# A two-layer graph network: the first table pair made and gathered by column halves

## The reference, cut to what matters

```python
h = jnp.maximum(_layernorm(x), 0.0)
# layer 1, n_f = h
feat = jnp.concatenate([n_f[edge_src], n_f[edge_dst]], axis=1)
e_hh = relu(feat[:256] @ W_hh + b_hh)
e_oo = relu(feat[256:1536] @ W_oo + b_oo)
e_ho = relu(feat[1536:] @ W_ho + b_ho)
logit = (concatenate([e_hh, e_oo, e_ho]) @ W_a + b_a)[:, 0]
alpha = softmax of logit over the edges of one dst        # segment_max, exp, segment_sum
z_f = segment_sum(alpha[:, None] * n_f[edge_src], edge_dst)
x = x + concatenate([relu([n_f, z_f][:128] @ W_hn + b_hn), relu([n_f, z_f][128:] @ W_on + b_on)])
# layer 2, h = relu(_layernorm(x)), c from the edge weights' sums and the degrees of the nodes
x = x + relu(((segment_sum(h[src] * c, dst)) * deg_in ** -0.5) @ W_1 + b_1)
```

## Time and profile before

| | us |
|---|---|
| median of 3 runs | 614.83 (609.78 to 616.64) |
| profiled execution, its own time | 611.59 |
| its span, first to last instruction | 609.6 |
| PE busy in the span | 541.2 (89%) |
| DVE busy | 417.3 (68%) |
| ACT busy | 213.3 (35%) |
| POOL busy | 163.8 (27%) |
| moved by DMA | 144.81 MB, mean 238 GB/s |

### The profile page before, as it was taken

How to read it: one execution, slowest core, us unless ns; L and a number is a source line. 1 busy time by engine, 2 the same in 40 slices (tenths; PEclk the granted TensorE clock), 3 DMA queues, 4 the chain that set the end, 5 groups by cost and what they waited for, 6 DMA issues and landing times.

```text
span 609.6 us, 7403 instructions
## 1 busy us (share of the span) xinstructions
PE 541.2 (89%) x2425; PEld 352.1 (58%) x2425; DVE 417.3 (68%) x744; ACT 213.3 (35%) x283; POOL 163.8 (27%) x157
## 2 busy tenths in 40 slices
PE   3868999999999979897339997898997999989996
PEld 2757888644444434342114444686665888868885
DVE  6948557447868799859397869755684277787134
ACT  3520427499463452100100157111444073216200
POOL 3110000177765375553267430000000101121000
PEclk9998999999999998999859999866998999999999
DMA  8975551599999999999969995140000736204002
GB/s 335 380 291 172 178 208 63 180 371 410 410 412 415 409 386 406 414 409 411 409 201 412 409 410 213 36 165 11 2 2 2 276 95 234 85 2 138 1 34 104
DMA packets 43780, 144.81 MB, mean 238 GB/s; under 512 B 5536, under 2 KB 5856, under 8 KB 43744
## 3 DMA queue, kind: packets, MB, share of 16 engines
q1 hardware_dynamic: 22000, 69.22, 30.9%
q0 software_dynamic: 18560, 67.13, 28.1%
q10 hardware_dynamic: 3184, 7.99, 3.5%
HBM read 131.70 MB, written 12.62 MB: 237 GB/s over the span
## 4 chain that ended last, share of the span: by engine, by line
PE 40%; DVE 24%; DMA 17%; issue 6%; POOL 5%; ACT 5%; DVEq 2%; ACTq 1%; POOLq 0%
PE banks L1080 19%; DMA rows<-table,ids_i 13%; PE banks L1243 7%; PE banks L1172 6%; DVE masked L791 5%; POOL rows L435 5%; DVE rows L769 5%; DVE rows L770 4%; PE banks L1260 3%; PE banks L1190 3%; DMA lift_row<-liftT 2%; ACT pick_src L553 2%; ACT pick_src L557 1%; DMA lift<-lift_row 1%; DVE stats L671 1%
## 5 line engine op out<-in xcount | busy, mean ns | idle before, releaser
L435 POOL DMA_INDIRECT rows<-table,ids_i x124 | 140.4, 1132 | 183.6 <-DMA table<-stage 86.4
L1100 PE MATMUL banks<-w_raw,fT_raw 128*128 128x512 f32 x384 | 168.4, 598 | 10.1 <-DMA w_raw<-in_L_gnn_W_hn_dram 3.9
L1100 PEld LDWEIGHTS banks<-w_raw,fT_raw 128*128 128x128 f32 x384 | 73.0, 192 | 104.9 <-issue 92.3
L769 DVE TENSOR_TENSOR rows<-rows 128x1024 f32<-128x1024 f32 x62 | 75.7, 1220 | 47.2 <-DMA rows<-table,ids_i 47.0
L681 DVE TENSOR_TENSOR w_lo<-w_raw,w_hi 128x1024 fp32r<-128x1024 f32 x40 | 48.4, 1223 | 57.1 <-ACT w_hi L484 47.5
L1080 PE MATMUL banks<-w_hi,fT_hi 128*128 128x512 f32 x200 | 78.7, 393 | 8.1 <-DVE w_lo L681 7.2
L1080 PE MATMUL banks<-w_lo,fT_hi 128*128 128x512 f32 x200 | 78.3, 392 | 0.0
L1080 PE MATMUL banks<-w_hi,fT_lo 128*128 128x512 f32 x200 | 78.3, 391 | 0.0
L770 DVE SCALAR_TENSOR_TENSOR rows<-rows,wa_rep 128x1024 f32<-128x1024 f32 x62 | 76.0, 1225 | 2.1
L1143 PE MATMUL banks<-w_raw,fT_raw 128*128 128x512 f32 x128 | 58.4, 619 | 19.5 <-DVE xf L823 19.5
L484 ACT ACTIVATE w_hi<-w_raw 128x1024 fp32r<-128x1024 f32 x40 | 41.7, 1056 | 86.9 <-PE banks L1080 72.9
(11 more groups left out here) (164 smaller groups left out, 619.1 us busy)
## 6 DMA issues: line engine op xcount, KB each, us to landing
w_raw<-in_L_gnn_W_ho_dram SPq DMA_DIRECT2D x16, 512.0 KB, 7.7
table<-stage SPq DMA_DIRECT2D x32, 256.0 KB, 7.6
w_raw<-in_L_gnn_W_oo_dram SPq DMA_DIRECT2D x16, 512.0 KB, 6.8
w_raw<-in_L_gnn_W_on_dram SPq DMA_DIRECT2D x16, 512.0 KB, 5.5
w_raw<-in_L_gnn_W_hn_dram SPq DMA_DIRECT2D x16, 512.0 KB, 6.7
w_raw<-in_L_gnn_W_hh_dram SPq DMA_DIRECT2D x16, 512.0 KB, 7.3
w_raw<-in_L_gnn_W_dram SPq DMA_DIRECT2D x8, 512.0 KB, 3.9
lift<-lift_row ACTq DMA_DIRECT2D x7, 512.0 KB, 8.0
```

Source lines behind the costliest of these rows:

```text
L435: pool.indirect_dma_start(out=rows[:, slot, side, :], out_offset=None, in_=table[kind][side], in_offset=bass.IndirectOffsetOnAxis(ap=ids_i ...
L769: step(dve.tensor_tensor(rows[:, r, 0, :], rows[:, r, 0, :], rows[:, r, 1, :], ALU.add))
L1100: ins = pe.matmul(bank[j][:, :], fT_raw[:, k, m * P:(m + 1) * P], w_raw[:, c % SLOTS, n * H:(n + 1) * H], start=(k == 0), stop=(k == K - 1))
```

## The change

**Halves.** Chunks c < 16 take other slices of W_ho: chunk c loads rows k*128 of both W_top and W_bottom, but one column half of each (`chunk_rows`). So bank j = 2m + n now holds node block m of side n, and unit 0 makes the left halves of both tables, unit 1 the right ones. ACT copies the even banks of both units, DVE the odd ones with the bias, and two semaphores (`evac_act`, `evac_dve`) replace `evac`. SP stores unit 0's eight copies twice, first to new tensors `table_left` (rows of 2 KB), then to the left columns of the tables.

**Sixteen left halves.** Tiles 0, 2, ..., 30 (`LEFT`) are gathered in two parts. Once `table_left` has landed, POOL gathers the left halves (32 gathers of 256 KB), DVE sums them into `left_logit` after its w_lo of chunks 12 to 15, at c = 16, and at c = 19. After unit 1 `fetch` goes through tiles 0 to 61 as before, but takes right halves for the sixteen (from the table seen as rows of 2 KB, with indices 2*id + 1), and `lift_chunk` adds `left_logit`.

**What moves for it.** `dst_rep` lies over `h_edge` instead of `rows` and has 4 places, so the loads of its chunks 4 to 7 go from ACT to POOL, each behind a `member` chunk, and the h_edge gathers stand behind the left gathers and all member builds. DVE builds four members for each c from 4 to 11. The split of the edge weights (`split3`, `dst_q`) goes to c = 8. The words are loaded once, 7 loads instead of 14, on DVE at c = 19 and on PE before the HH transposes. `EDGES_BY`, and the places of lifts and maxima, are new; TOP's banks 0 and 1 are kept at c = 47. Two of four `hn_lo` leave the second round of spans and stand behind `adjT_lo`.

```diff
     def chunk_rows(c):
+        if c < 2 * K:
+            half, k = c // K, c % K
+            return W_ho.rearrange("(s r) d -> r s d", s=2)[k * P:(k + 1) * P, :, half * H:(half + 1) * H]
...
-        ROWS, REPS = 5, 6
+        ROWS, REPS = 5, 4
...
+        table_left = [nc.dram_tensor(f"table_left{s}", [N, H], F32, kind="Internal").ap() for s in range(2)]
...
+        LEFT = range(0, 32, 2)
+        NL = len(LEFT)
+        ITEMS = [(i, 0) for i in LEFT] + [(i, 1 if i in LEFT else 2) for i in range(TE)]
+
         EDGES_BY = [0] * C_BOT
         for c in range(20, C_BOT):
-            if c < 28:
-                n = 2 * (c - 19)
-            elif c < 32:
-                n = 16 + c - 27
-            elif c < 36:
-                n = 20 + 2 * (c - 31)
+            if c < 36:
+                n = 36 * (c - 19) // 16
             elif c < 44:
-                n = 28 + 13 * (c - 35) // 8
+                n = 36 + 12 * (c - 35) // 8
             elif c < 52:
-                n = 41 + 5 * (c - 43) // 8
+                n = 48 + 6 * (c - 43) // 8
...
-        FETCH_AFTER = (26, 30, 35, 40, 45, 55, 61)
-        MAX_AFTER = (27, 32, 37, 42, 47, 57, 62)
+        FETCH_AFTER = (25, 29, 33, 38, 42, 47, 58)
+        MAX_AFTER = (27, 31, 36, 40, 44, 49, 61)
...
+                for j in range(8 if u == 0 else 0):
+                    evacuated(sp, j)
+                    sp.dma_start(table_left[j % 2][j // 2 * P:(j // 2 + 1) * P, :], stage[:, j, :]).then_inc(left_stored, 16)
                 for j in range(8):
                     e = 8 * u + j
-                    sp.wait_ge(evac, e + 1)
+                    evacuated(sp, e)
                     m, n = j // 2, j % 2
...
+            for r in range(REPS, NC):
+                pool.wait_ge(member_done, r - REPS + 1)
+                dst_rep_load(pool, r)
+            pool.wait_ge(left_stored, 16 * STAGE)
+            pool.wait_ge(words_ready, 1)
+            for k in range(NL):
+                fetch(k)
+            pool.wait_ge(member_done, NC)
             pool.wait_ge(h_out, 16)
...
-                fetch(i)
+                fetch(NL + i)
...
-                for j in range(8):
+                for j in range(0, 8, 2 if u < 2 else 1):
...
-            def edge(i):
-
-                r = i % ROWS
-                dve.wait_ge(row_in[r], (i // ROWS + 1) * 32)
-                step(dve.tensor_tensor(rows[:, r, 0, :], rows[:, r, 0, :], rows[:, r, 1, :], ALU.add))
-                dve.scalar_tensor_tensor(rows[:, r, 0, :], rows[:, r, 0, :], 0.0, wa_rep[:, :], ALU.max, ALU.mult,
-                                         accum_out=logit[:, i:i + 1]).then_inc(edge_done, 1)
+            def edge(k):
+
+                (i, part), r = ITEMS[k], k % ROWS
+                cols = slice(0, D if part == 2 else H)
...
+                dve.wait_ge(row_in[r], (k // ROWS + 1) * 32)
...
-            split3(w_col, ids_f[:, 2, :])
...
-            dve.wait_ge(words_ready, 1)
-            words = [dve.value_load(pair_word[0:1, q % WORDS:q % WORDS + 1], min_val=0, max_val=4096 ** 2 - 1)
-                     for q in range(2 * WORDS)]
...
+            early = {12: 3, 13: 6, 14: 9, 15: 12, 16: 14, 19: NL}
             for c in range(4, C_BOT):
+                if c == K + 3:
+                    evacuate(0)
                 if c not in RAW:
                     lo(c)
-                if c < 20:
-                    for part in (2 * (c - 4), 2 * (c - 4) + 1):
-                        build_member(part // B, part % B)
+                if c < 19:
+                    for k in range(early.get(c - 1, 0), early.get(c, 0)):
+                        edge(k)
+                if c - 4 < NC:
+                    for b in range(B):
+                        build_member(c - 4, b)
...
-                if c == C_HH + 3:
+                if c == C_TOP + 2 * K - 1:
                     keep_top(range(2))
...
+            pe.wait_ge(words_ready, 1)
+            words = [pe.value_load(pair_word[0:1, q:q + 1], min_val=0, max_val=4096 ** 2 - 1) for q in range(WORDS)]
+
             transpose_edges(0)
```

164 lines of the change are left out of this document (100 added, 64 removed).

## The result

The changed kernel takes 622.67 us (median of 11 runs, 617.39 to 628.09), the kernel before in the same comparison 616.44 (609.78 to 618.52, 11 runs): ratio 1.0099, 95% interval 1.0053 to 1.0145. It is slower by 1.0%, where 600.5 and faster were forecast. In all that follows a median is taken over all runs of a kernel, and a ratio over its fast runs alone, those within 1.5% of its fastest. The profiled execution took 625.53 us, span 623.6, against 611.59 and 609.6: 14.0 us more.

The account below looks back on a forecast made before the run. The middle was taken as bound twice: gathers fill the DMA engines, and DVE's order passes that to PE. Gains 6.3 + 3.1 + 3.5 less 1 of clock, 12 us off 611.6, plus 0.9: 600.5 us, range 588 to 612.

Parts of the forecast that it names:

- Step 1: DVE's early program: without word loads w_lo of chunk 4 starts at 34.8; PE's first pass ends at 62.4, not 71.
- Step 2: DVE's member builds and splitting: it copies its banks only at 65 us; left tables stand at 72.
- Step 3: Left gathers: 32 at 1.24 us; DVE's copies end at 117.4, before 115.6, so the 8.6 us gained are spent.
- Step 4: h_edge gathers beside the last table stores: second pass's first gather at about 126, plus 6.5 us (bounds 1.8 and 8).
- Step 5: Half rows in the second gather pass: 8.4 MB less gains 20.5 us; POOL's pace charged 3 us (bounds 0 and 7).
- Step 6: New tile counts in DVE's order: unit 3 copied at 236, HH starting at 308 instead of 314.35, 6.3 us sooner.
- Step 7: PE's seven word loads moved ahead of the transposes, where PE waits anyway: the 3.13 us before 377.49 go.
- Step 8: Span stage: DVE free when HH ends, and two hn_lo moved behind adjT_lo; counted as 3.5 of 4.6 us.
- Slower, the left gathers hold PE: Left gathers delay fT_raw and free banks, deciding from 1.67 us a gather; 621 us at 1.99; chance 0.08.
- Thin gain: POOL needs 1.43 us a gather in the left pass, 5.3 us more, and 2 more behind it: 608; chance 0.20.

Follow-up runs that it names:

- small parts alone: Kernel before with words loaded once and late, edge-weight split behind chunk 8, two hn_lo moved, no halves: 608.04 us, ratio 0.9899.
- the layout alone: Changed kernel without its left pass: whole rows everywhere, tile counts of before, the rest as changed: 609.07 us, ratio 0.9837.
- the changed kernel once more: Changed kernel run again without any edit, for a second profile: 624.05 us, ratio 1.0142.
- the left pass alone: Changed kernel gathering whole rows behind the second unit, of which DVE sums the right half for the sixteen tiles: 633.85 us, ratio 1.0266.
- one side left out: Kernel before, with tiles 0, 2, ..., 30 gathering only side 0 in whole rows: 605.70 us, ratio 0.9855.
- the run with POOL 4 tiles ahead: Half-row kernel with POOL at most 4 tiles ahead of DVE instead of 5, until tile 33: 609.36 us, ratio 0.9848.
- the free run with eight left halves: Changed kernel with left halves for tiles 0 to 14 only, h_edge gathers behind tile 40, no added pauses: 608.31 us, ratio 0.9901.
- with 4 tiles ahead: The free run with eight left halves, but POOL at most 4 tiles ahead of DVE until tile 19: 608.70 us, ratio 0.9900.
- the half-row kernel: Kernel before, tiles 0, 2, ..., 30 gathering and summing only left halves, right halves left out: 601.23, 619.69, 621.01, 624.56 us.
- 3 ahead, twice: POOL at most 3 tiles ahead of DVE instead of 5: half-row kernel 616.94 us (1.0057), changed kernel 634.92 us (1.0406).
- the pauses: Changed kernel with POOL waiting before tiles 6, 12, 18, 24 and 30 until DVE is 2 tiles behind: 635.61 us, ratio 1.0367.

## Why the prediction was wrong, step by step

The span was to fall by 12 and rose by 14.0. By the runs' medians the parts are: small parts and layout -6, left pass with the h_edge gathers behind it +25, half rows behind the turn -10, together +9, where the changed kernel itself measured +6.2 and +9.9. The runs of one kernel spread over 8 us and more, so each part is known to a few us only.

*Step 1* held. w_lo of chunk 4 starts at 34.61, PE does not stand, and the run with the small parts alone gives 6 us of it.

*Step 2* held: DVE's first copy at 63.98 (65), left tables at 71.48 (72).

*Step 3* failed, and is the largest miss. The gathers took 1.26 us each in the median, but 36.0/32 + 0.30 = 1.43 in the mean, the upper bound I had named, and DVE came late by 4 us: the 14th tile was summed at 114.84, not 111, and the copies were done at 121.0, not 117.4. What I left out is what 32 gathers do to PE's second pass, which took 54.8 us (64.7 to 119.5) and not 43.5. I had priced the left pass by when its sums are done, with PE as a bystander. Until 92 us PE's products follow each other in 0.23 us; then they come singly:

```profile
92.05 0.39 PE L1138 MATMUL banks<-w_hi,fT_hi 128*128 128x512 f32 x1
93.95 0.39 PE L1138 MATMUL banks<-w_hi,fT_hi 128*128 128x512 f32 x1 [0.71 <-issue]
95.41 0.47 PE L1138 MATMUL banks<-w_hi,fT_hi 128*128 128x512 f32 x1 [0.35 <-issue]
111.83 0.40 PE L1138 MATMUL banks<-w_hi,fT_hi 128*128 128x512 f32 x1 [0.69 <-issue]
101.77 1.22 DVE L716 TENSOR_TENSOR w_lo<-w_raw,w_hi 128x1024 fp32r<-128x1024 f32 x1
```

It is not its weights that PE lacked: the last w_lo (bottom row) was ready at 103.0, and the chunk that needs it, the last 24 products, begins at 111.83. The gaps are "issue", so the profile shows nothing that PE waited for. They go with the length of the left pass:

| profiles | gaps of PE in its second pass | the pass takes |
|---|---|---|
| six with 32 left gathers | 13 to 20, in sum 5.0 to 10.8 us | 54.8 to 66.1 us |
| three with 16 | none, none and one | 43.0 to 44.2 us |
| the layout alone | none | 43.0 us |

In the changed kernel once more the granted clock also fell, to 0.65 from 104 to 130 us, and the pass took 65 us. ACT's wait of 11.91 us at 94.04 is of the same stretch; with 16 gathers ACT does that step at 86.11 after 4.08.

*Step 4* put the h_edge gathers at plus 6.5, bounds 1.8 and 8. Between two single profiles it is 8.6 (135.23 against 126.64 without them), over all of them 6 to 9. The mechanism, stores held behind gathers, is seen in two profiles and in two others not, as told above. Together with step 3 the turn is 23.4 us after that of the layout alone (24.0 in the run with the left pass alone), where I had 15 (8.6 and 6.5).

*Step 5* is the term that should have carried the gain. The bytes are worth what I said when a gather goes with them (one side left out: 9 to 11 us in the end). Halving rows keeps the gathers, and POOL's pace is then the bound, not one "as near as DMA": the first 64 gathers behind the turn end at 224.7, 1.40 us each. A half row at that pace brings 256 KB in 1.40 us, 187 GB/s, a whole one twice that; the windows show 321 to 353 GB/s in place of 410 for 85 us. At their mean of 335 that is 85 x 75 = 6.4 MB, 15.5 us at 410, where I charged 3. This is an estimate: some of the shortfall is weights that SP, with late signals, did not ask for. That the DMA engines can take such a mix of halves and wholes faster shows in the run with POOL 4 tiles ahead: 380 GB/s from 160 to 180 us, the table stores of unit 2 among them.

*Step 6*: copies of unit 3 at 253.47, not 236. Of the 17.5 us the turn has 9.2, the tiles 8.3. The step's own arithmetic (equal bytes, so 36 tiles like 28) fell with step 5, since 36 tiles are 72 gathers where 28 are 56. HH at 330.4, not 308.

*Step 7* held: 3.9 us less between HH and the maxima product. Its seven loads cost PE 2.93 us of "issue" ahead of the transposes, at 327.05 and so on HH's path, which the sum had at nothing. *Step 8* failed: moving two hn_lo gave nothing that shows. From the maxima product to the z products it is 73.4 us before, 74.1 with the small parts alone, 78.3 in the changed kernel, the last at a lower granted clock and not by a wait, as the rows above show.

*The rivals.* "Slower, the left gathers hold PE" was given 0.08 and was to decide from 1.67 us a gather. It came true at 1.43, by way of PE's own gaps more than of DVE's sums: these were 4 us late in the first profile, and in the second DVE itself waited 6.90 us for PE (until 122.97). "Thin gain" had POOL's 1.43 right and led to 608: half of the answer.

*What stays open* is why PE's products and signals come late. The signals did (chunk 26 at 55 to 79 us in place of 48.3) in seven profiles, in all of which POOL had issued gathers at 1.33 to 1.39 us each, with no wait of over 0.7 us, for 47 us and more. They did not where POOL had waits. But the free run with eight left halves has such a stretch too (42 gathers from 112.0 to 170.2 us), and its signals are in time, as they are with 4 tiles ahead (34 gathers in 49 us); and one run in four of the half-row kernel took 601. So POOL's unbroken issue goes with it. Real breaks ended it in the three profiles whose kernel has late signals without them (3 ahead, twice, and the pauses); the two with eight left halves say nothing here, since the free run is in time too. It is not shown to be enough, and what in the chip stands in the way was not tried.

## What to carry to other kernels

Count a gather's saving in instructions of the issuing engine as well as in bytes: at 1.25 to 1.4 us each, gathers of 256 KB cannot fill the DMA engines, and splitting a transfer in two to save half of one side saves nothing where POOL is near its pace. A pass put into "idle" time of POOL and DMA can be paid elsewhere, here by PE's own products and its signals; try it at half its length first. A stand of PE that is new in a profile is not yet the loss: look whether another engine would have been late all the same. And where two profiles differ in one stage, compare busy time and granted clock before looking for a wait.
